# Attention scores from stacked fp16 halves that pass through DRAM, taken one iteration later, and the residual sum on GpSimd

## The chip, the cores and the metric

One NeuronCore of a Trainium2 chip runs the kernel. The time is that of one execution on the device, in microseconds (us). TensorE multiplies, VectorE and ScalarE work on tiles, GpSimd does small tile work and indirect transfers, SyncE starts most of the other transfers. Profile names: PE is TensorE's matmul, PEld its weight load, DVE is VectorE, ACT ScalarE, POOL GpSimd, SP SyncE; a q behind a name is that engine's own sequencer.

## The reference

The input x has 2 batches of 2048 tokens by 512. What is computed, cut to what matters:

```python
x = x + tanh(g_xattn[0]) * xattn(layernorm(x), ctx, ...)      # 16 heads of 32, 128 context rows
x = x + tanh(g_ffn[0]) * ffn(layernorm(x), ...)               # 8 experts of width 256, top 2, and a shared one of 512

q = query @ Wq.T + bq;  k = key @ Wk.T + bk;  v = value @ Wv.T + bv
att = einsum('bhsd,bhtd->bhst', q, k) / sqrt(32)              # masked by pad_mask and subsq_mask
out = einsum('bhst,bhtd->bhsd', softmax(att), v)
```

## The kernel before, in words

**Three passes.** Pass 1 takes 32 tiles of 128 tokens (tile n belongs to batch n % 2) through layernorm, query projection, attention, the residual sum, a second layernorm, the router and, for the tiles of batch 1, the shared expert. Pass 2 takes 71 slots of 128 gathered rows through the experts. Pass 3 sums everything up for the output and does the shared expert of batch 0. The change is in pass 1 and in what is set up ahead of it.

**The pipeline of pass 1.** Every engine has one `body(J, v)`, run once per iteration; iteration i is J = i // 2, v = i % 2. A stage with lag L works on tile i - L, and `tile(J, v, lag)` gives the tile n, its number j in its batch and its buffer u. The lags are LQ = 2 (transpose the normed tile, project it to q), LS = 3 (scores, row maxima, exp), LV = LS + 1 (probabilities transposed, times values), LX1 = LS + 2 (second half of the normalisation, residual sum, statistics), LX2 = LS + 3 (second layernorm, transpose, router), LR and LK for ranks and lists, and LU, LG, LD, LB for the shared expert, all counted from LX2. The order inside an iteration is the order in which `body` is written, engine by engine; semaphores tie the engines together. Work that belongs to no tile hangs on iteration numbers: weight peaks on DVE in iterations 3 to 14, and in iterations 16 to 31 the split of expert weights into fp16 halves, `split_high` on ACT when v = 0 and `split_low` on DVE (line 1097) when v = 1. PLAN_IT = NT + LK - 1 is the iteration in which DVE plans pass 2.

**Query projection.** x is split into an fp16 high and low half (`x_hi` on ACT, line 647; `x_lo` on DVE, line 942). `queries` (lines 1340 to 1342) makes q transposed, channels on partitions, in PSUM bank 0: four column blocks, each of 4 x 3 fp16 products over 128 rows. ACT then writes `q_t` in fp32 with four instructions that apply scale and bias (line 688) and raises `q_ready`, which releases bank 0 and the scores.

**Scores.** `scores(k)` (line 1301) is called for k = 0 and k = 2 and makes two groups of 4 heads each time, into banks 2 and 3. One head is one fp32 product over the 32 rows of that head; heads of row group g and g + 1 alternate. An fp32 product is two records in the trace, so 16 heads are 32 records a tile.

**Behind them.** DVE adds the mask and takes row maxima (`maxima(k)`, line 887) for four groups. GpSimd subtracts the maxima for three groups (`shift(k)`, line 527), ACT takes the exponentials (lines 629 and 681). PE transposes probabilities (`turn_probs`, line 1217), ACT copies them (`take_probs`, line 622), PE multiplies by values (`mix_values`, line 1325), DVE normalises (`normalise`, lines 899 and 901). DVE makes x1 = attn * gate + x (line 937), raising `x1_ready`; then statistics (line 951). `keys_and_values` in iteration 2 writes `k_t` and `vaug` (lines 867 and 872).

**GpSimd's order.** `shift(0)`, mask, `shift(1)`, mask, `shift(2)`, two small chains for the layernorms (lines 546 to 556), then two indirect transfers that scatter token numbers (line 565). **SP's order** in an iteration: store x1 (line 401), store the normed rows (line 405), load x (line 412), load x again for the residual (line 419), shared expert traffic.

## Time and profile before

| | |
|---|---|
| median of 3 runs | 1089.7 us (1083.06 to 1090.62) |
| the profiled execution's own time | 1085.73 us |
| its span in the profile | 1083.5 us |
| PE busy over the span | 93% |
| DVE busy | 72% |
| granted TensorE clock, mean over the span | 0.96 of full speed |

The span runs from the first to the last instruction that the profiler saw; the time of the execution has 2.2 us more around it. Pass 1 ends near 600 us. A busy share is an average over three passes with different limits, so the argument reads pass 1 by stretches. PE's records are pipelined: a matmul of 219 ns can be followed by the next one 56 ns later, so what an instruction costs PE is the distance between starts and not its own duration.

### The profile page before, as it was taken

To read this page: it belongs to the slowest core of one execution; us is meant where nothing else is said; L and a number is where in the kernel's file an instruction comes from. 1 tells how busy PE (TensorE), PEld (TensorE's weight loads), DVE (VectorE), ACT (ScalarE), POOL (GpSimd) and SP (SyncE) were. 2 spreads that over 40 slices of the span, in tenths; PEclk is the share of its full clock that TensorE was granted. 3 is DMA by queue.
4 is the path that set the end of the run, shared out by engine and by line. 5 is a ranking of instruction groups with operands and counts; after the bars stand their busy time and mean duration, and the time that the engine had idled before them with its cause. 6 is when DMAs were issued, how large, how long until landed. Compare 5 with 4: busy or idle time off the path is not lost.

```text
span 1083.5 us, 31212 instructions
## 1 busy us (share of the span) xinstructions
PE 1012.0 (93%) x10160; PEld 778.7 (72%) x10161; DVE 775.1 (72%) x2795; ACT 500.1 (46%) x1010; POOL 425.3 (39%) x606
## 2 busy tenths in 40 slices
PE   5889899999999999999996599999999999989997
PEld 4678889888899888899984355555555555578885
DVE  4577888887898888888776566666666666545656
ACT  2456555456566566666542344444444444311111
POOL 4333355454555565554533222222212221045553
PEclk9787899999999999999998799999999999999999
DMA  9502565742455433236225243333333334169987
GB/s 369 222 21 90 211 135 100 111 103 73 54 103 109 109 100 89 60 81 184 89 82 135 68 128 117 116 115 113 113 114 116 116 116 145 60 182 329 303 292 262
DMA packets 76754, 147.30 MB, mean 136 GB/s; under 512 B 20912, under 2 KB 23088, under 8 KB 73872
## 3 DMA queue, kind: packets, MB, share of 16 engines
q1 hardware_dynamic: 46800, 68.11, 25.4%
q0 software_dynamic: 12896, 35.58, 11.3%
q10 hardware_dynamic: 16992, 42.74, 10.2%
q8 instruction: 41, 0.67, 0.3%
q14 instruction: 25, 0.20, 0.1%
HBM read 94.04 MB, written 52.35 MB: 135 GB/s over the span
## 4 chain that ended last, share of the span: by engine, by line
PE 75%; DVE 9%; issue 6%; ACT 4%; DMA 3%; POOL 2%; another core or an unknown queue 1%; SPq 0%; ACTq 0%; POOLq 0%; DVEq 0%
PE bank L1217 10%; PE bank L1225 9%; PE bank L1226 9%; PE bank L1227 9%; PE bank L1325 8%; PE bank L1301 5%; PE bank L1275 5%; PE bank L1277 4%; PE bank L1276 4%; PE bank L1285 2%; PE bank L1342 2%; PE bank L1340 2%; PE bank L1341 2%; DVE arena L887 2%; PE bank L1287 2%
## 5 line engine op out<-in xcount | busy, mean ns | idle before, releaser
L1275 PE MATMUL bank<-arena,weights 128*128 128x128 f16 x1024 | 185.3, 225 | 13.5 <-DVE arena L1018 8.7
L1277 PE MATMUL bank<-arena,weights 128*128 128x128 f16 x1024 | 185.1, 225 | 0.0
L1276 PE MATMUL bank<-arena,weights 128*128 128x128 f16 x1024 | 185.1, 225 | 0.0
L1217 PE MATMUL bank<-ident,arena 128*128 128x128 f32 (+1 forms) x1336 | 179.5, 270 | 2.5 <-DMA arena<-normed_rows,arena 1.9
L579 POOL DMA_INDIRECT arena<-normed_rows,arena x71 | 69.1, 973 | 250.1 <-PE bank L1217 225.0
L1217 PEld LDWEIGHTS bank<-ident,arena 128*128 128x128 f32 (+1 forms) x1336 | 143.8, 141 | 23.8 <-DMA arena<-normed_rows,arena 2.5
L527 POOL TENSOR_TENSOR arena<-arena 128x512 f32<-128x512 f32 x96 | 101.0, 1052 | 142.7 <-DVE arena L887 135.1
L1325 PE MATMUL bank<-arena 128*128 128x33 f32 x1024 | 137.3, 280 | 7.6 <-ACT arena L622 7.6
L1325 PEld LDWEIGHTS bank<-arena 128*128 128x128 f32 x1024 | 131.4, 200 | 14.7 <-ACT arena L622 12.2
L887 DVE CUSTOM_DVE_ANT_0 arena<-bank,arena 128x128 f32<-128x128 f32 x512 | 116.9, 284 | 31.2 <-PE bank L1301 31.2
L622 ACT ACTIVATE arena<-bank 128x512 f32<-128x512 f32 x128 | 75.9, 593 | 115.5 <-PE bank L1217 108.2
L1275 PEld LDWEIGHTS bank<-arena,weights 128*128 128x128 f16 x1024 | 103.4, 101 | 21.1 <-DVE arena L1018 8.8
L1225 PE MATMUL bank<-weights,arena 128*128 x284 | 107.7, 379 | 1.7 <-DVE arena L1153 1.6
L1226 PE MATMUL bank<-weights,arena 128*128 x284 | 107.6, 379 | 0.0
L1227 PE MATMUL bank<-weights,arena 128*128 x284 | 107.6, 379 | 0.0
L1276 PEld LDWEIGHTS bank<-arena,weights 128*128 128x128 f16 x1024 | 103.5, 101 | 2.0
L1277 PEld LDWEIGHTS bank<-arena,weights 128*128 128x128 f16 x1024 | 103.7, 101 | 0.0
L1340 PE MATMUL bank<-arena 128*128 128x128 f16 x512 | 93.9, 227 | 3.0 <-issue 1.6
L1159 DVE TENSOR_SCALAR arena<-bank,arena,w_back 128x512 f32<-128x512 f32 x71 | 57.5, 810 | 54.2 <-PE bank L1227 54.2
L1341 PE MATMUL bank<-arena 128*128 128x128 f16 x512 | 93.8, 227 | 1.1 <-issue 1.1
L1342 PE MATMUL bank<-arena 128*128 128x128 f16 x512 | 93.6, 227 | 0.0
L1301 PE MATMUL bank<-arena 32*128 32x128 f32 x1024 | 78.9, 295 | 9.4 <-ACT arena L688 7.5
(196 smaller groups left out, 2268.9 us busy)
## 6 DMA issues: line engine op xcount, KB each, us to landing
expert_rows<-arena ACTq DMA_DIRECT2D x71, 256.0 KB, 2.2
arena<-in_x SPq DMA_DIRECT2D x64, 256.0 KB
x_rows<-arena SPq DMA_DIRECT2D x48, 256.0 KB, 5.4
arena<-x_rows SPq DMA_DIRECT2D x48, 256.0 KB, 3.8
weights<-in_w_gu ACTq DMA_DIRECT2D x8, 1024.0 KB, 7.0
normed_rows<-arena SPq DMA_DIRECT2D x32, 256.0 KB, 5.6
out<-weights ACTq DMA_DIRECT2D x32, 256.0 KB, 4.5
weights<-in_w_down ACTq DMA_DIRECT2D x4, 1024.0 KB, 13.5
```

What stands on the lines that cost most here:

```text
L887: last = d.tensor_tensor_reduce(score[u][:, hh * T:(hh + 1) * T], bank[2 + k % 2][:, h * T:(h + 1) * T], mask_bias[u], 1.0, LOWEST, ALU.ad ...
L1217: last = t.transpose(dst[:, c * P:(c + 1) * P], src[:, c * P:(c + 1) * P], (ident16 if src.dtype == F16 else ident)[:, :])
L1225: t.matmul(dst, hi[:, rows], w_hi(c), start=(c == 0), stop=False)
L1226: t.matmul(dst, hi[:, rows], w_lo(c), start=False, stop=False)
L1227: last = t.matmul(dst, lo[:, rows], w_hi(c), start=False, stop=(c == chunks - 1))
L1275: t.matmul(at, shared(c, part, 0, dc), x_hi_c, start=(c == 0), stop=False)
L1276: t.matmul(at, shared(c, part, 0, dc), x_lo_c, start=False, stop=False)
L1277: last = t.matmul(at, shared(c, part, 1, dc), x_hi_c, start=False, stop=(c == EC - 1))
L1301: mm = t.matmul(bank[2 + g % 2][:, c * T:(c + 1) * T], q_t[u][rows, c * P:(c + 1) * P], k_t[rows, c, u, :], start=True, stop=True)
L1325: last = t.matmul(bank[A_BANK][:, at:at + D + 1], probs_t[k % 2][:, h * P:(h + 1) * P], vaug[:, u, k * HG + h, :], start=True, stop=True)
L1340: t.matmul(dst, wq[:, 0, at:at + P], x_hi[:, xs], start=(ci == 0), stop=False)
L1341: t.matmul(dst, wq[:, 0, at:at + P], x_lo[:, xs], start=False, stop=False)
```

## The change

It does these things:

- q is no longer written in fp32. ACT writes the fp16 high half of q, scaled (`q_halves`), straight from bank 0, and DVE writes the low half at the start of the next iteration, which is now what raises `q_ready`. SP stores both halves to DRAM (`query_halves`) and, once that has landed, loads them back as `q_stack`: for each head 96 rows, high, low, high.
- The keys go the same way once, in iteration 2, with rows high, high, low, and with a scale that is found from their largest value by `top_peaks`, `all_peaks` and `scale_of`.
- A head's score is one fp16 product over the 96 rows. `scores` makes one group of 4 heads per call and is called four times, (0) and (1) at the place of the old (0), (2) and (3) at that of the old (2). The scale goes into the exponentials.
- bq is added on PE: a fp16 product over 64 rows, `bq_half` by `bias_row`, closes each of the four column blocks of `queries`.
- LS becomes 4, so all later stages come one iteration later.
- The attention gate is multiplied into the values and their bias once, so x1 is a plain sum, and it is made on GpSimd at the start of the iteration, ahead of `shift(0)`.
- SP's order in an iteration: store q, load x twice, store x1, load the stack, store the normed rows.
- Arena addresses move, two semaphores are merged into one at the layernorm and in pass 2, and load_down(1) is issued in iteration NT + 2.

```diff
-        LQ, LS = 2, 3
+        LQ, LS = 2, 4
@@ SP, body
+                n, j, u = tile(J, v, LQ + 1)
+                if live(n, NT):
+                    hold(sp, sp_passed, (q_ready, n + 1))
+                    sp.dma_start(q_dram[u].rearrange("a p n -> p a n"), q_halves.rearrange("p (a n) -> p a n", a=2)).then_inc(q_out[u], 16)
...
+                n, j, u = tile(J, v, LQ + 1)
+                if live(n, NT):
+                    hold(sp, sp_passed, (q_out[u], 16 * (j + 1)))
+                    hold(sp, sp_passed, (s_done, group(n - 2, EC - 1)))
+                    stack(q_stack[u], q_dram[u], (0, 1, 0), q_stacked[u])
...
+            def stack(dst, src, parts, done):
+
+                for at, part in enumerate(parts):
+                    sp.dma_start(dst[at * D:(at + 1) * D, :].rearrange("d (h n) -> d h n", h=HG),
+                                 src[part].rearrange("(h d) n -> d h n", h=HG)).then_inc(done, 16)
...
+                if it == KEYS_IT:
+                    sp.wait_ge(k_lo_set, 1)
+                    sp.dma_start(k_dram.rearrange("a p n -> p a n"), k_halves.rearrange("p (a n) -> p a n", a=2)).then_inc(k_out, 16)
+                    sp.wait_ge(k_out, 16)
+                    stack(k_stack, k_dram, (0, 0, 1), k_stacked)
@@ GpSimd, body
+                n, j, u = tile(J, v, LX1)
+                if live(n, NT):
+                    hold(pool, pool_passed, (res_here[u], 16 * (j + 1)))
+                    need(pool, x1_out[u], 16 * j)
+                    need(pool, xn2_ready, n - 1)
+                    pool.wait_ge(attn_done[0], n + 1)
+                    pool.wait_ge(attn_done[1], n + 1)
+                    g.tensor_tensor(x1[u], attn, x_res[u], ALU.add).then_inc(x1_ready, 1)
@@ ACT, body
-                    need(act, s_done, group(n - 2, EC - 1))
-                    for c in range(EC):
-                        last = a.activation(q_t[u][:, c * P:(c + 1) * P], bank[0][:, c * P:(c + 1) * P], ACT.Identity,
-                                            scale=w_back[:, 0:1], bias=bq_s[:, c:c + 1])
-                    last.then_inc(q_ready, 1)
+                    hold(act, act_passed, (q_out[(v - LQ - 1) % 2], 16 * (j + u)))
+                    a.activation(q_halves[:, 0:E], bank[0][:, :], ACT.Copy, scale=Q_DOWN).then_inc(q_hi_ready, 1)
@@ DVE, normalise and body
+                        need(dve, x1_ready, n)
...
+                n, j, u = tile(J, v, LQ + 1)
+                if live(n, NT):
+                    dve.wait_ge(q_hi_ready, n + 1)
+                    d.scalar_tensor_tensor(q_halves[:, E:2 * E], bank[0][:, :], Q_DOWN, q_halves[:, 0:E], ALU.mult, ALU.subtract).then_inc(q_ready, 1)
...
-                    d.scalar_tensor_tensor(x1[u5], attn, gate[:, 0:1], x_res[u5], ALU.mult, ALU.add).then_inc(x1_ready, 1)
@@ PE, body
-                        for c in range(EC):
-                            for g in (k, k + 1):
-                                rows = slice(g * D, (g + 1) * D)
-                                mm = t.matmul(bank[2 + g % 2][:, c * T:(c + 1) * T], q_t[u][rows, c * P:(c + 1) * P],
-                                              k_t[rows, c, u, :], start=True, stop=True)
+                        pe.wait_ge(q_stacked[u], 16 * PARTS * (j + 1))
+                        pe.wait_ge(k_stacked, 16 * PARTS)
+                        need(pe, max_done, group(n, k - 2))
+                        for h in range(HG):
+                            q_at, k_at = (h * EC + k) * P, ((h * EC + k) * B + u) * T
+                            last = t.matmul(bank[2 + k % 2][:, h * T:(h + 1) * T], q_stack[u][0:STACK, q_at:q_at + P],
+                                            k_stack[0:STACK, k_at:k_at + T], start=True, stop=True)
+                        last.then_inc(s_done, 1)
...
-                                last = t.matmul(dst, wq[:, 1, at:at + P], x_hi[:, xs], start=False, stop=(ci == EC - 1))
+                                t.matmul(dst, wq[:, 1, at:at + P], x_hi[:, xs], start=False, stop=False)
+                            last = t.matmul(dst, bq_half[:, co * P:(co + 1) * P], bias_row[:, :], start=False, stop=True)
```

How the order moves is shown at two places. First TensorE in a late iteration of pass 1, at the second call for scores and at the projection. In the kernel before, L1217 is a transpose, L1301 a score, L1285 the shared expert and L1340 to L1342 the projection:

```order
L1217 MATMUL bank<-ident,arena 128x128 x3
L302 REGISTER_ALU [waits q_ready]
L1301 MATMUL bank<-arena 128x128 [waits max_done]
L1301 MATMUL bank<-arena 128x128 x7
L1285 MATMUL bank<-weights,arena 128x512
```

In the changed kernel at the same place L1365 is a score and L1351 the shared expert; further on, L1404 to L1406 are the projection and L1407 is the bias:

```order
L1365 MATMUL bank<-arena 128x128 [waits max_done]
L1365 MATMUL bank<-arena 128x128 x3
L317 REGISTER_ALU [waits k_stacked,q_stacked1]
L1365 MATMUL bank<-arena 128x128 [waits max_done]
L1365 MATMUL bank<-arena 128x128 x3
L1351 MATMUL bank<-weights,arena 128x512
...
L1404 MATMUL bank<-arena 128x128
L1405 MATMUL bank<-arena 128x128
L1406 MATMUL bank<-arena 128x128
L1407 MATMUL bank<-bias_row,bq_half 128x128
L1404 MATMUL bank<-arena 128x128
```

The count of products stays 8 here and 16 a tile, their wait on `q_ready` has become one on the transfer, and a bias product stands between the column blocks of the projection, four times a tile.

Second GpSimd, at the seam between two iterations. Before, L562 and L565 are the token scatter, L527 is `shift`, L537 the mask:

```order
L562 COPY arena<-token_no 128x1 [waits rows_out0]
L565 DMA token_of_row<-arena 36864x1 [waits row_ready,tok_ready]
L565 DMA token_of_row<-arena 36864x1
L527 TENSOR_TENSOR arena<-arena 128x512 [waits max_done]
L537 TENSOR_TENSOR arena<-arena,pad_keep 128x128 [waits max_done,sub_set]
```

In the changed kernel L611 and L614 are the scatter, L577 is the residual sum and L568 is `shift`:

```order
L611 COPY arena<-token_no 128x1 [waits rows_out1]
L614 DMA token_of_row<-arena 36864x1 [waits row_ready,tok_ready]
L614 DMA token_of_row<-arena 36864x1
L577 TENSOR_TENSOR arena<-arena 128x512 [waits attn_done0,xn2_ready,attn_done1,x1_out1,res_here1]
L568 TENSOR_TENSOR arena<-arena 128x512 [waits max_done]
```

The sum with its five waits stands between the scatter of the iteration before and `shift(0)`.

## Rows read from the trace of the kernel before

**Rows 1.** The page: busy time of each engine, and TensorE's granted clock in 40 slices

```profile
PE 1012.0 (93%) x10160; PEld 778.7 (72%) x10161; DVE 775.1 (72%) x2795; ACT 500.1 (46%) x1010; POOL 425.3 (39%) x606
PEclk9787899999999999999998799999999999999999
```

**Rows 2.** Stretches of pass 1: start, end, length, busy us by engine, clock, DMA, GB/s

```profile
45.00:64.00 19.00, 18.98 (x133) 17.66 (x131) 8.62 (x42) 7.45 (x17) 5.68 (x9) 0.55 0.35 136
399.00:414.80 15.80, 15.78 (x223) 15.03 (x222) 14.00 (x64) 9.20 (x21) 7.07 (x10) 1.00 0.37 99
414.80:431.00 16.20, 15.80 (x188) 13.64 (x188) 12.89 (x69) 11.14 (x22) 10.46 (x18) 1.00 0.30 93
550.00:600.00 50.00, 33.42 (x389) 27.78 (x388) 36.72 (x157) 14.82 (x28) 16.78 (x25) 0.88 0.43 107
```

**Rows 3.** Groups by line over the span: busy us, mean ns, idle before and releaser

```profile
L1301 PE MATMUL bank<-arena 32*128 32x128 f32 x1024 | 78.9, 295 | 9.4 <-ACT arena L688 7.5 <-DVE arena L887 1.5
L688 ACT ACTIVATE arena<-bank,bq_s,w_back 128x128 f32<-128x128 f32 x128 | 47.9, 455 | 13.4 <-PE bank L1342 13.3
L937 DVE SCALAR_TENSOR_TENSOR arena<-arena,gate 128x512 f32<-128x512 f32 x32 | 38.9, 1216 | 1.2
L942 DVE SCALAR_TENSOR_TENSOR arena<-bank,arena 128x512 f16<-128x512 f32 x32 | 22.0, 686 | 17.1 <-ACT arena L647 17.1
```

**Rows 4.** Timeline of PE around both score calls of one iteration: start, length

```profile
414.14 0.63 PE L1217 MATMUL bank<-ident,arena 128*128 128x128 f32 x4
415.91 0.23 PE L1275 MATMUL bank<-arena,weights 128*128 128x128 f16 x1
415.98 0.22 PE L1276 MATMUL bank<-arena,weights 128*128 128x128 f16 x1
416.14 0.22 PE L1276 MATMUL bank<-arena,weights 128*128 128x128 f16 x1
421.28 0.49 PE L1217 MATMUL bank<-ident,arena 128*128 128x128 f32 x3
421.70 1.16 PE L1301 MATMUL bank<-arena 32*128 32x128 f32 x16
421.70 0.38 PE L1301 MATMUL bank<-arena 32*128 32x128 f32 x2
422.79 0.39 PE L1285 MATMUL bank<-weights,arena 128*128 128x512 f16 x1
```

**Rows 5.** Waits of PEld from 60 to 550 us

```profile
PEld bank L1301 <- ACT arena L688: 7.4, 13, 2.9
```

**Rows 6.** Timeline of DVE, ACT and POOL at one place of the loop, and an earlier L937

```profile
413.19 1.49 ACT L688 ACTIVATE arena<-bank,bq_s,w_back 128x128 f32<-128x128 f32 x4
415.19 0.42 DVE L901 TENSOR_TENSOR arena<-bank,arena 128x256 f32<-128x256 f32 x1
420.08 1.05 POOL L527 TENSOR_TENSOR arena<-arena 128x512 f32<-128x512 f32 x1
401.71 1.05 POOL L527 TENSOR_TENSOR arena<-arena 128x512 f32<-128x512 f32 x1
402.00 1.73 DVE L937 SCALAR_TENSOR_TENSOR arena<-arena,gate 128x512 f32<-128x512 f32 x1
418.07 0.75 DVE L937 SCALAR_TENSOR_TENSOR arena<-arena,gate 128x512 f32<-128x512 f32 x1
```

**Rows 7.** DMA issues: count, KB each, median us to landing

```profile
x_rows<-arena SPq DMA_DIRECT2D x48, 256.0 KB, 5.4
weights<-in_w_down ACTq DMA_DIRECT2D x4, 1024.0 KB, 13.5
```

**Rows 8.** Timeline: the keys on DVE, and the first scores of the first two tiles

```profile
26.25 1.64 DVE L867 TENSOR_SCALAR arena<-bank,bk_s 128x256 f32<-128x256 f32 x4
33.68 1.16 PE L1301 MATMUL bank<-arena 32*128 32x128 f32 x16
44.78 1.82 PE L1301 MATMUL bank<-arena 32*128 32x128 f32 x16 [1.86 <-ACT arena L688]
```

More of the change, by code:

```diff
@@ L680, in body @@
                         sc = score[u][:, h * T:(h + 1) * T]
-                        last = a.activation(sc, sc, ACT.Exp, bias=peaks_neg[:, h - H + HG:h - H + HG + 1])
+                        last = a.activation(sc, sc, ACT.Exp, scale=score_scale[:, :], bias=peaks_neg[:, h - H + HG:h - H + HG + 1])
                     last.then_inc(exp_done, 1)
@@ L1249, in _, with values @@
             last.then_inc(kv_mm, 1)
-            def values():
+            def values(b):
                 pe.wait_ge(v_in, 16)
-                for b in range(B):
-                    for ci in range(EC):
-                        last = t.matmul(bank[6 + b][:, :], ctx_s[:, ci, b * T:(b + 1) * T], wv_s[:, ci, :],
-                                        start=(ci == 0), stop=(ci == EC - 1))
-                last.then_inc(kv_mm, 1)
+                for ci in range(EC):
+                    last = t.matmul(bank[6 + b][:, :], ctx_s[:, ci, b * T:(b + 1) * T], wv_s[:, ci, :],
+                                    start=(ci == 0), stop=(ci == EC - 1))
+                if b == B - 1:
+                    last.then_inc(kv_mm, 1)
             def it_is_first(n, k):
```

264 lines of the change are left out of this document (153 added, 111 removed).

## The prediction

> **What bounds the kernel now.** I read the page first, for busy shares and clock, then pass 1 by stretches, then the groups by line, then the timeline around the changed places, and last the waits and the transfers.
>
> The page has PE busy for 93% of the span and DVE for 72% [rows 1]. That says little of where a saved microsecond counts, so I go to stretches. In a late stretch of the loop two iterations take 15.80 and 16.20 us, PE is busy for 15.78 and 15.80 us of them at full clock, DVE for 14.00 and 12.89, ACT for 9.20 and 11.14, GpSimd for 7.07 and 10.46 [rows 2]. PE bounds the loop there, and what it saves per tile is saved from the iteration, as long as DVE does not take over about 2 us lower. Early in pass 1 it is mixed: from 45 to 64 us PE is busy all the time at a granted clock of 0.55, about its lower level of 1.2 GHz, and the clock slices 2 to 7 of the page are below full [rows 1, 2]. At the end of the pass, from 550 to 600 us, PE is busy 33.42 of 50 us [rows 2]: the pipeline drains through chains of small steps.
>
> **Scores on PE.** What counts is the distance between starts. In a late iteration the last fp32 pass ahead of the second score call begins at 421.28 + 0.49 - 0.27 = 421.50 (a pass is recorded for 0.27), and the first product behind the call at 422.79: 1.29 us, of which 0.11 is that pass's own distance, so the call takes 1.18 [rows 4]. The first call is from 414.14 + 0.63 - 0.27 = 414.50 to 415.91, 1.41 less 0.11, or 1.30. Together 2.48 us a tile; the group agrees, 78.9 us over 32 tiles is 2.47 [rows 3]. The fp16 products are 0.055 apart (415.98 to 416.14 is three of them) [rows 4], and 128 columns over 96 rows are the same stream, so 16 heads take 0.89. Scores alone save 1.59 us a tile.
>
> **The bias on PE.** Four products more a tile are 0.22 us if they stream like the others. But they are products over 64 rows between products over 128, and no such product is in this trace. The nearest row is the switch to the scores' 32 rows. Going in, the last pass starts at 421.50 and the first score at 421.70, 0.20 where passes are 0.11 apart: 0.09 lost. The first scores are recorded for 0.38 where the rest have about 0.28, another 0.10. Coming out, the last pass starts at 421.70 + 1.16 - 0.27 = 422.59 and the next product at 422.79, again 0.20 and 0.09 lost [rows 4]. A visit thus costs 0.28 over its stream. If a visit of 64 rows costs the same, the bias takes 4 x (0.28 + 0.055) = 1.34 us a tile. Lower bound 0.22, no cost of switching. Upper bound: the 0.20 is a fixed gap whatever streams, then 4 x (0.20 + 0.10 + 0.20 - 0.055) = 1.78. I take 1.34, since the loss over the stream is what the row shows both ways. The Trainium skill, TensorEngine Tiling (Array Packing), Key Properties, says that changing the tiling mode drains TensorE. The trace agrees as far as it goes: the loss is there on entry and on exit of the 32-row scores. By that rule this change takes 2 score visits away and puts 4 bias visits in; without it the bias would be 0.22.
>
> PE per tile: -2.48 + 0.89 + 1.34 = -0.25 us; bounds -1.37 and +0.19. The loop is bound by PE as in rows 2 for some 18 iterations (those of 16 to 33), so -4 us, bounds -25 and +3.
>
> **The early iterations (4 to 15).** The same per tile, at a clock that is partly half, and PE or DVE waits in turn. There q's way over ACT goes from the path: PEld waited 7.4 us for L688 in 13 places from 60 to 550 us, most of them early [rows 5], and ACT's four instructions, 47.9 us over 32 tiles [rows 3], or 1.5 a tile, become one copy of about 0.6. DVE gives up L937, 38.9 us in all at 1.216, and takes q's low half, priced by L942 at 0.686 [rows 3]: 17 us less busy, half a microsecond a tile, and DVE is near the bound there. I take -8 us together; bounds 0 (the waits return on another semaphore) and -20 (7.4 of waits, 12 iterations at 0.5 of DVE, the rest PE at the lower level).
>
> **The residual sum on GpSimd.** One more instruction like L527, 1.05 us [rows 6]. It stands ahead of `shift(0)` and behind the scatter, and everything on GpSimd behind it moves back by 1.05 when it is late: the exponentials, the mask, and x1_ready with the store of x1 and SP's queue behind that. In the row, `shift(0)` starts at 420.08 [rows 6], so the sum would end near 421.1; statistics need it only behind `maxima(2)`, near 424. GpSimd is busy 10.46 of 16.20 at most [rows 2]; I cost it at nothing, covered by PE's 15.8. If that cover is gone it costs up to 1.05 an iteration. L937 was 1.73 us when it began beside an L527 (401.71 to 402.76) and 0.75 alone [rows 6]. The Trainium skill, SBUF — State Buffer, on the two sides of ports, has this as an exclusive lock between a GpSimd operation and a DVE operation with two SBUF inputs; the row agrees. By it the new sum can hold up DVE operations that read two SBUF tiles (the weight split), by 1 us each time at most; the removed L937 was the one that met it.
>
> **The stack through DRAM.** ACT's q starts at 413.19 and would be done at 413.8; DVE comes to q's low half behind L901, at 415.61, and ends at 416.3 [rows 3, 6], with L942 as the price. The store is priced by x_rows, 256 KB in 5.4 us [rows 7], to 421.7. Behind it on SP wait the stack's three loads, then the store of normed rows. The loads are 384 KB in rows of 1 KB; at 5.4 us plus 0.7 for issuing three they land near 427.8. The first scores of the next iteration start one iteration after 414.82, near 430.8. So the transfers fit with about 3 us to spare, and cost nothing in the loop. Bounds: 0, and where 1 MB loads run (13.5 us to landing [rows 7], iterations 7 to 11) some 8 us late, two or three times.
>
> **Start and the extra iteration.** Before, the keys were made at 26.25 to 27.9 and the first scores ran at 33.68, the second tile's at 44.78 [rows 8]. Now the keys need a reduction, a transpose and a spread on PE, the scale, a high half on ACT and a low half on DVE: I estimate ready at about 36. A store and a load of 5.4 each put the keys in place at 47, and q's first stack, which SP issues behind them, at about 50. The first scores then run in iteration 4 at about 50, where before the second tile's ran at 44.78. The work of that iteration is one stage lighter, so this is not 16 us but 50 - 44.8 plus PE's own 2.4 of scores not yet done, less what PE can do meanwhile: +6, bounds 0 and +12. At the other end one iteration more drains. It holds no new work, PE is idle a third of the time there [rows 2]: +3, bounds +1 and +8.
>
> **Sum.** -4 - 8 + 6 + 3 = -3 us against the profiled execution's 1085.73, so 1083. That execution lies 4 us under the median of the runs shown, 1089.7, which others are compared with; on that scale I forecast 1087. Passes 2 and 3 have only addresses and semaphores changed: 0. All lower bounds together would be -44 (-25, -20, 0, +1), all upper ones +43 (+3, 0, +20 for late stacks, +12, +8); neither is likely.
>
> **The rivals.** (A) The 64-row products stream without a loss. For: accumulation goes on in the same bank and the row shown is of 32 rows in alternating groups. Against: both edges of those rows lose. PE then saves 1.37 a tile: 18 x 1.37 = 25, early -13 (the 8 above, and 12 iterations at 1.12 more of which four tenths count), start and drain +9: -29, 1060. It also needs DVE to keep up, with 14.00 - 0.5 of about 14.6 us. (B) Slower: the stack is late. Its place is `scores(0)` on PE, which then waits for a transfer. From q's high half to the landed stack takes 14 us against 17 us to the next scores, and it decides from the point where store and load take 3 us more than priced, by 1 KB rows, by SP being held at x1_ready behind GpSimd's scatter, or by other transfers. Were it 4 us more in all iterations, 1 us x 30 = 30 less overlap of some odd ones, say +22: 1109. For: three transfers in series and a queue that waits in order. Against: the DMA engines' share is 0.30 to 0.37 in rows 2. (C) The switch costs the upper bound: +0.19 instead of -0.25, 0.44 x 30 = +13: 1100. (D) GpSimd's sum, shift and ACT's exponentials become the ring that closes the loop: GpSimd is idle a third of the time, so at most +0.5 an iteration: 1102 or so.
>
> **Chances.** Forecast 0.36, A 0.25, B 0.17, C 0.14, D 0.08. This measurement can tell about 1% from no change. Of the forecast 0.29 lies within 1%, 0.05 under it and 0.02 over; A is faster; B is slower; C and D are half within 1%, half slower. That gives faster 0.30, same 0.40, slower 0.30. The range must take in A and B: 1056 to 1108. The forecast's own range is 1075 to 1098.
>
> **What would show it.** A score group of 512 records at 0.055 apart, about 0.9 us a tile. Around each bias product: the distance from the product before it to the one behind it, 0.39 if I am right, 0.11 in rival A, 0.50 or more in C. Pairs of late iterations of 31.5 us instead of 32.0; 29.3 in A. PE waiting for a transfer ahead of the scores would be B, GpSimd's sum as what ACT's exponentials wait for would be D. First scores near 50 us. I am wrong if late iterations keep or gain time for a reason other than PE's switches, or if pass 1 ends more than 10 us off 597.

## The result, and the profile after

The changed kernel takes 1130.97 us, median of 4 runs (1128.83 to 1134.22). The kernel before takes 1086.64 in its 4 runs beside it. The ratio is 1.041, with a 95% interval of 1.036 to 1.046: 4% slower, outside the forecast range and slower than any rival. Ratios here and below are formed from the fast runs alone, which leaves out four of the seven runs of before in the second group and four of the 23 in the fourth, so the medians given there do not yield them.

The page after, as [rows 1] for before: busy time by engine, and the granted clock in 40 slices.

```profile
PE 1020.4 (90%) x9779; PEld 774.0 (69%) x9780; DVE 791.4 (70%) x2809; ACT 496.5 (44%) x915; POOL 470.8 (42%) x643
PEclk9877699999999999999997799999999999999999
```

PE has 381 records fewer and is still busy 8 us longer. To see where the 45 us of span come in, I put marks into pass 1: the first row maximum on DVE, the last one, and the last addition into `seen`, which ends the pass. Timeline of DVE in the kernel before:

```profile
34.99 0.28 DVE L887 CUSTOM_DVE_ANT_0 arena<-bank,arena 128x128 f32<-128x128 f32 x1
...
551.55 0.28 DVE L887 CUSTOM_DVE_ANT_0 arena<-bank,arena 128x128 f32<-128x128 f32 x1
...
589.97 0.15 DVE L926 TENSOR_TENSOR seen<-seen,arena 128x8 f16<-128x8 f16 x1
```

And after:

```profile
57.32 0.29 DVE L961 CUSTOM_DVE_ANT_0 arena<-bank,arena 128x128 f32<-128x128 f32 x1 [5.77 <-PE bank L1365]
...
590.80 0.29 DVE L961 CUSTOM_DVE_ANT_0 arena<-bank,arena 128x128 f32<-128x128 f32 x1
...
634.15 0.15 DVE L1005 TENSOR_TENSOR seen<-seen,arena 128x8 f16<-128x8 f16 x1
```

The start is 22.3 us longer (57.3 against 35.0), the 32 tiles from first to last maximum take 16.9 more (533.5 against 516.6), the tail 4.9 (43.3 against 38.4). That makes 44.2, and passes 2 and 3 add 1. These are marks and not three causes: by DVE's statistics of the input tiles the pass is 5.8 us longer up to the sixteenth tile, 18.7 from there to the last, and 19.7 behind it.

**What PE does per tile came out better than forecast.** Two score calls of four heads and one bias product in a late iteration, timeline of PE after:

```profile
404.22 0.61 PE L1365 MATMUL bank<-arena 96*128 96x128 f16 x8
404.67 0.22 PE L1341 MATMUL bank<-arena,weights 128*128 128x128 f16 x1
...
410.56 0.22 PE L1406 MATMUL bank<-arena 128*128 128x128 f16 x1
410.71 0.23 PE L1407 MATMUL bank<-bias_row,bq_half 64*128 64x128 f16 x1
410.87 0.23 PE L1404 MATMUL bank<-arena 128*128 128x128 f16 x1
```

Eight scores take 0.45 us, so a tile 0.90, as forecast. Around the bias product it is 0.31 from the product before to the one behind, where I forecast 0.39 and rival A 0.11. So PE saves 2.48 - 0.90 - 4 x (0.31 - 0.055) = 0.56 us a tile.

**Yet late iterations are longer.** Stretches of eight late iterations, from DVE's statistics of one input tile to those of the eighth behind it (start, end, length, busy us of PE, PEld, DVE, ACT, POOL, clock). Before:

```profile
381.10:508.80 127.70, 125.90 (x1634) 114.58 (x1634) 107.45 (x526) 81.34 (x173) 70.02 (x108) 1.00 0.40 101
```

After:

```profile
396.20:533.30 137.10, 127.90 (x1543) 114.78 (x1542) 109.24 (x525) 80.44 (x149) 82.54 (x116) 0.96 0.56 124
```

An iteration went from 15.96 to 17.14 us. PE was idle 1.8 us in the eight, now 9.2, and its clock is no longer full. The waits of that stretch after:

```profile
PE bank L1388 <- ACT arena L679: 9.2, 6, 2.1
```

L1388 is `mix_values`, L679 `take_probs`. One such wait is followed back in the timelines. GpSimd after, from the end of one iteration into the next:

```profile
430.95 0.22 POOL L601 TENSOR_SCALAR arena<-arena 128x1 f32<-128x1 f32 x1 [1.68 <-DVE arena L1080]
...
433.25 1.10 POOL L614 DMA_INDIRECT token_of_row<-arena  x1 [0.85 <-POOL arena L611]
434.67 0.96 POOL L614 DMA_INDIRECT token_of_row<-arena  x1 [0.31 <-issue]
435.66 1.27 POOL L577 TENSOR_TENSOR arena<-arena 128x512 f32<-128x512 f32 x1
436.88 1.04 POOL L568 TENSOR_TENSOR arena<-arena 128x512 f32<-128x512 f32 x1
```

ACT after, behind it:

```profile
437.95 0.72 ACT L686 ACTIVATE arena<-arena,score_scale 128x512 f32<-128x512 f32 x1 [2.18 <-POOL arena L568]
...
438.92 1.99 ACT L804 ACTIVATE weights<-weights,w_scale  x1
440.81 0.71 ACT L686 ACTIVATE arena<-arena,score_scale 128x512 f32<-128x512 f32 x1
441.43 0.58 ACT L679 ACTIVATE arena<-bank 128x512 f32<-128x512 f32 x1
```

And PE:

```profile
442.06 1.08 PE L1388 MATMUL bank<-arena 128*128 128x33 f32 x8 [2.06 <-ACT arena L679]
```

Read it as one chain: DVE's last statistics of an iteration release GpSimd (430.95), which makes the scale of the layernorm, scatters twice, makes the sum and only then the shift; that releases ACT's first exponential, behind which stand the weight split, the second exponential and, in ACT's order, `take_probs(2)` of the tile before; PE needs that for `mix_values(2)`, and everything DVE does later in the iteration hangs on PE. The sum lies in this chain with its full 1.27 us.

The chain was there before, which I had overlooked. The chain of waits of the kernel before, from 380 to 394 us, start and length of each step:

```profile
387.19 0.97 POOL token_of_row L565
388.18 1.06 POOL arena L527
...
390.24 1.46 ACT weights L747
...
392.03 0.61 ACT arena L629
392.65 0.49 ACT arena L622
393.19 1.08 PE bank L1325 x8
```

It had hardly any slack: PE waited for L622 four times in the eight iterations, 1.6 us in all. That GpSimd was idle 5.74 of 16.20 us [rows 2] said nothing of what this chain could take in.

**Idle PE can cost twice.** Between 463.2 and 498.8 us PE waited once, 2.06 us ahead of 475.54. Stretches around this gap, after:

```profile
472.00:475.50 3.50, 1.48 (x23) 1.24 (x20) 3.32 (x30) 3.50 (x7) 2.59 (x5) 1.00 0.94 172
475.50:479.00 3.50, 3.46 (x21) 3.40 (x22) 1.76 (x6) 1.09 (x3) 0.45 (x1) 0.51 0.70 203
479.00:482.50 3.50, 3.50 (x32) 2.88 (x30) 1.41 (x3) 2.70 (x6) 1.16 (x4) 0.51 0.00 0
482.50:486.00 3.50, 3.50 (x54) 3.15 (x52) 1.12 (x3) 1.37 (x3) 2.38 (x3) 1.00 0.01 0
```

The clock goes from full to 0.51, about the 1.2 GHz level, for 7 us in which PE is busy, and back. These two iterations took 35.6 us; the two before them, with gaps of 2.06 and 0.60 and no fall of the clock, 33.5. So one gap of this length was followed by a fall and one was not, and these rows do not show what decides it.

### The profile page after: what moved, and what is told of

It is laid out like the page before. It is cut to its first block, busy times and chain, and to the rows that moved or that the text cites. A ratio compares the mean times of both kernels' runs of the same rounds, so it can differ in the third digit from the quotient of the medians.

```text
span 1128.8 us, 31111 instructions
## 1 busy us (share of the span) xinstructions
PE 1020.4 (90%) x9779; PEld 774.0 (69%) x9780; DVE 791.4 (70%) x2809; ACT 496.5 (44%) x915; POOL 470.8 (42%) x643
## 4 chain that ended last, share of the span: by engine, by line
PE 71%; DVE 8%; DMA 6%; issue 6%; POOL 4%; ACT 3%; SPq 1%; ACTq 0%; DVEq 0%; POOLq 0%; another core or an unknown queue 0%
PE bank L1283 9%; PE bank L1388 8%; PE bank L1291 8%; PE bank L1292 8%; PE bank L1293 8%; PE bank L1341 4%; PE bank L1343 4%; PE bank L1342 4%; PE bank L1404 3%; PE bank L1405 2%; PE bank L1406 2%; PE bank L1351 2%; PE bank L1352 2%; PE bank L1353 2%; PE bank L1365 2%
## 5 line engine op out<-in xcount | busy, mean ns | idle before, releaser
L1283 PE MATMUL bank<-ident,arena 128*128 128x128 f32 (+1 forms) x1336 | 182.2, 272 | 4.6 <-DVE arena L989 2.2
L1342 PE MATMUL bank<-arena,weights 128*128 128x128 f16 x1024 | 185.8, 226 | 0.0
L1388 PE MATMUL bank<-arena 128*128 128x33 f32 x1024 | 142.4, 285 | 34.9 <-ACT arena L679 29.4
L1388 PEld LDWEIGHTS bank<-arena 128*128 128x128 f32 x1024 | 133.6, 202 | 46.8 <-ACT arena L679 38.6
L568 POOL TENSOR_TENSOR arena<-arena 128x512 f32<-128x512 f32 x96 | 101.7, 1060 | 92.0 <-DVE arena L961 91.8
L679 ACT ACTIVATE arena<-bank 128x512 f32<-128x512 f32 x128 | 75.8, 592 | 134.9 <-PE bank L1283 124.0
L1404 PE MATMUL bank<-arena 128*128 128x128 f16 x512 | 107.5, 240 | 3.9 <-DVE arena L1015 3.7
L1405 PE MATMUL bank<-arena 128*128 128x128 f16 x512 | 107.0, 239 | 0.0
L1406 PE MATMUL bank<-arena 128*128 128x128 f16 x512 | 106.8, 239 | 0.0
L1342 PEld LDWEIGHTS bank<-arena,weights 128*128 128x128 f16 x1024 | 103.9, 101 | 2.1
L686 ACT ACTIVATE arena<-arena,score_scale 128x512 f32<-128x512 f32 x96 | 69.1, 720 | 68.5 <-POOL arena L568 68.5
```

What stands on the lines that cost most here:

```text
L1283: last = t.transpose(dst[:, c * P:(c + 1) * P], src[:, c * P:(c + 1) * P], (ident16 if src.dtype == F16 else ident)[:, :])
L1342: t.matmul(at, shared(c, part, 0, dc), x_lo_c, start=False, stop=False)
L1388: last = t.matmul(bank[A_BANK][:, at:at + D + 1], probs_t[k % 2][:, h * P:(h + 1) * P], vaug[:, u, k * HG + h, :], start=True, stop=True)
L1404: t.matmul(dst, wq[:, 0, at:at + P], x_hi[:, xs], start=(ci == 0), stop=False)
L1405: t.matmul(dst, wq[:, 0, at:at + P], x_lo[:, xs], start=False, stop=False)
L1406: t.matmul(dst, wq[:, 1, at:at + P], x_hi[:, xs], start=False, stop=False)
```

## The experiments

Fifteen kernels. Medians of before differ from chip to chip (1091, 1120, 1089 and 1130 us for the four groups below), so kernels are compared by their ratio to before on the same chip. The changed kernel itself ran only beside the before of 1086.64, so its 1.041 is set against ratios of other chips. Where a ratio cannot tell, I use the end of pass 1 in the one profiled execution (590.0 before, 634.2 after). That is a single execution, and the four runs of rows_later_sum lie 15 us apart. The chips themselves differ behind pass 1 above all: passes 2 and 3 took 491 to 497 us in the traces of the first and third group and 514 to 531 in those of the others, while probs_first_before ended pass 1 at 592.1 on the chip where before takes 1130.

### First group: one part of the change each

**lag_only** adds to before nothing but the extra iteration.

```diff
-        LQ, LS = 2, 3
+        LQ, LS = 2, 4
@@ SP: the mask's load goes from lag 0 to lag LS - 3
```

> The kernel before with LS = 4 and nothing else (the load of the mask moves with it). Theory 1 (the extra iteration is paid whole): an iteration at each end is nearly its full length of about 15 us, so 1087 + 10 to 20, about 1101, and late pairs of iterations stay near 31.9 us. Rival (the forecast's own pricing: the iteration holds no new work, +3 to +5): 1091. A second rival, that the shift by one of the shared expert's work against the weight split is what costs: late pairs grow to 33 or more and the time is near 1115.

Measured: ratio 1.0135 (1.0102 to 1.0167), 15 us: theory 1. So the extra iteration alone is worth five times my 3 us. Its eight late iterations take 124.60 us, less than before. The cost lies elsewhere. The whole of pass 1, lag_only:

```profile
0.00:611.30 611.30, 559.04 (x6507) 505.19 (x6508) 459.53 (x2155) 327.75 (x689) 298.14 (x453) 0.92 0.49 117
```

Before:

```profile
0.00:590.00 590.00, 547.42 (x6507) 493.30 (x6509) 463.25 (x2155) 326.16 (x689) 285.58 (x452) 0.95 0.46 121
```

The same 6507 records of PE take it 11.6 us more, and it is idle 9.7 us more. (The profiled execution was the slowest of the four, 4 us over their median, so it shows 21 us where the median has 15.) The added iteration stands behind the last input tile. From that tile's statistics to the end of the pass, before:

```profile
508.80:590.00 81.20, 73.27 (x890) 63.44 (x890) 58.66 (x294) 38.07 (x82) 35.29 (x51) 0.96 0.41 114
```

And lag_only:

```profile
507.70:611.30 103.60, 92.03 (x1059) 81.54 (x1058) 68.97 (x355) 44.63 (x96) 42.86 (x62) 0.88 0.44 118
```

That is 22.4 us more, with 169 records more, 3.6 us more of idle PE and a clock of 0.88 instead of 0.96. Ahead of it the gains and losses cancel: up to the sixteenth input tile lag_only is 12 us quicker, from there to the last 11 slower. Two of its gaps, of 3.9 us up to 185.2 and of 3.4 up to 291.9, have no release that the profile names, and the clock was at half for 5 us behind the first and 14 behind the second. Whether they belong to the extra iteration is open.

**sum_dve** takes the changed kernel and puts the sum back on DVE, where it was.

```diff
@@ GpSimd
-                    g.tensor_tensor(x1[u], attn, x_res[u], ALU.add).then_inc(x1_ready, 1)
@@ DVE, ahead of maxima(1)
+                    d.scalar_tensor_tensor(x1[u5], attn, 1.0, x_res[u5], ALU.mult, ALU.add).then_inc(x1_ready, 1)
```

> The changed kernel with the residual sum on VectorE at its old place. Theory 1 (the loop is closed by a chain of GpSimd's scatter, the sum, shift(0), ScalarE's exponential, the weight split's high half, the next exponential and take_probs(2), for which TensorE waits ahead of mix_values(2)): 1.3 us leaves that chain in each pair of iterations and the VectorE operation that lasted 2.45 us beside the sum returns to 0.7, so a late pair falls from 33.5 to near 31.5 us and the time to about 1131 - 16 - some early gain = 1112. Rival (TensorE's own work or the transfers set the pace): within 3 us of 1131.

Measured: 1.019 (1.0148 to 1.0232), 1110.33 us, theory 1: half of the whole loss goes away with one instruction a tile. Its eight late iterations:

```profile
388.70:515.70 127.00, 122.33 (x1538) 110.36 (x1538) 109.76 (x534) 80.21 (x148) 69.76 (x108) 1.00 0.59 134
```

PE is 3.6 us less busy than before and 4.7 idle instead of 1.8, of which it waits 3.5 for `take_probs`; for the other 1.2 the profile names no release. Most of what the scores save is lost in the same wait, and the iteration is nearly as long as before.

**bias_128** pads the bias product from 64 to 128 rows with zeros, so its stream and its result are the same.

```diff
-        bq_half = sb("bq_half", [2 * D, E], F16)
+        bq_half = sb("bq_half", [P, E], F16)
@@ the same for bq_raw, bias_row and the host's zero rows
```

> The changed kernel with the bias product over 128 rows, 64 of them zero, so that TensorE keeps one tiling mode. The distance around a bias product falls from 0.31 to 0.11 us, 0.8 us a tile. Theory 1 (in the late loop TensorE waits once per pair for a chain that does not hold the bias): of the 26 us that come off TensorE in 32 tiles less than half shows, 1131 to 1120. Rival (TensorE sets the pace everywhere): 1105.

Measured: 1.0293 (1.0253 to 1.0332), theory 1: some 13 of the 26 us that PE no longer spends show. Timeline of PE in bias_128:

```profile
405.18 0.22 PE L1406 MATMUL bank<-arena 128*128 128x128 f16 x1
405.23 0.22 PE L1407 MATMUL bank<-bias_row,bq_half 128*128 128x128 f16 x1
405.29 0.22 PE L1404 MATMUL bank<-arena 128*128 128x128 f16 x1
```

Now it is 0.11 from product to product across the bias, against 0.31. So the loss of 0.20 a visit is that of going from 128 rows to 64 and back, and it costs nothing to avoid. The Trainium skill, TensorEngine Tiling (Array Packing), Key Properties, says that changing the tiling mode drains TensorE. The rows agree: 0.31 us around the product over 64 rows, 0.11 around the padded one.

**late_split** moves ACT's weight split of every second iteration behind `take_probs(3)`.

```diff
-                elif v == 0:
-                    split_high(J)
                 exponent(1)
                 take_probs(2)
...
                 take_probs(3)
+                if not isinstance(J, int) and v == 0:
+                    split_high(J)
```

> The changed kernel with ScalarE's high half of the weight split (1.99 us, once in each of 8 pairs of iterations) issued behind take_probs(3) instead of ahead of the second exponential. Theory 1 (that instruction stands in the chain TensorE waits for): TensorE's wait of 2 us ahead of mix_values(2) goes, 8 pairs fall from 33.5 to about 31.7 us, 1131 - 14 = 1117. Rival (the wait only moves, to take_probs(3) or to VectorE's low half): 1131 within 3.

Measured: 1.0347 (1.0305 to 1.0389), not told apart from the changed kernel for certain: the rival. The chain of waits of late_split shows why:

```profile
458.44 1.28 POOL arena L577
...
462.21 1.05 POOL arena L568
...
463.92 0.59 ACT arena L679
```

With the split gone from between the exponentials, ACT waits for GpSimd's second shift instead. The chain goes one step further along GpSimd. Eight late iterations of this trace take 132.0 us against 137.1, with 4.2 us of waits for `take_probs` and 3.0 for row maxima, so the split did stand in the way there; yet its pass 1 ends at 638.2, later than the changed kernel's 634.2, and I did not follow where the rest went.

### Second group: do the parts add, where in the chain, and the start

On this chip before took 1119.69 us (1103 to 1124), and intervals are wide.

**sum_dve_bias** is sum_dve and bias_128 together.

> The changed kernel with two edits at once: the sum of attention and x back on DVE where it was, and the bias product over 128 rows. Alone the first gave 1110.3 and the second 1121.3, against 1131.0. Theory 1 (the sum keeps ACT's exponentials and so PE waiting, the bias costs PE its switches; two separate costs): the gains add, some 20.6 + 9.7, so 1101, late pairs of iterations near 30.9 us (31.8 less four products that lose 0.2 each, in two tiles). Theory 2 (with PE 0.8 us a tile quicker, the chain over GpSimd, ACT and PE closes the loop again): 1107 to 1110, late pairs stay at 31.6 or more with PE waiting longer for ACT's take_probs.

Measured: 1.0164 (0.999 to 1.034); pass 1 ends at 611.0, sum_dve's at 615.5. Eight late iterations take 126.5 us against 127.0, and PE waits 6.7 us for `take_probs` instead of 3.5: theory 2. Much of the 0.8 us a tile that the bias no longer costs goes into the wait.

**sum_later** keeps the sum on GpSimd and puts it behind `shift(0)`.

```diff
+                shift(0)
                 n, j, u = tile(J, v, LX1)
                 if live(n, NT):
...
                     g.tensor_tensor(x1[u], attn, x_res[u], ALU.add).then_inc(x1_ready, 1)
-                shift(0)
```

> The changed kernel with the sum still on GpSimd, but behind shift(0) instead of ahead of it. Theory 1 (its place in GpSimd's order is what costs: 1.3 us ahead of the shift that ACT's first exponential waits for): most of the 21 us come back, 1114 to 1119, late pairs near 32.0. Theory 2 (what costs is that it shares the way to the tiles with DVE, whose instructions beside it take 2 us longer, wherever it stands): 1125 to 1135, late pairs 33 or more.

Measured: 1.0471 (1.032 to 1.063), pass 1 ends at 633.3: nothing gained that can be told. Here my two theories were badly cut. The instructions of DVE beside the sum are no longer stretched (L998 took 1.56 us in the mean of four in late iterations of the changed kernel, 0.684 in each of them here), and still nothing is gained. The timeline of GpSimd in sum_later has the reason, as in late_split: the sum now stands ahead of the second shift, and that one is waited for as well.

```profile
455.40 1.05 POOL L568 TENSOR_TENSOR arena<-arena 128x512 f32<-128x512 f32 x1
456.40 1.28 POOL L578 TENSOR_TENSOR arena<-arena 128x512 f32<-128x512 f32 x1
...
459.02 1.04 POOL L568 TENSOR_TENSOR arena<-arena 128x512 f32<-128x512 f32 x1
```

**pool_sum_before** is the kernel before with the sum on GpSimd ahead of `shift(0)`, otherwise as it was. It leaves out the gate on the attention.

> The kernel before with one part of the change alone: the sum of attention and x as a plain sum on GpSimd ahead of shift(0), off DVE. The gate on the attention is left out. Theory 1 (the chain GpSimd, ACT, PE already stood in the chain of waits of before, so 1.3 us more in it come out as time whatever the scores cost): 1100 to 1112, late pairs of 33 to 33.5 instead of 31.9. Theory 2 (only because PE has become quicker per tile does the sum cost): 1087 to 1095, late pairs of 32.0 to 32.4.

Measured: 1.0228 (1.007 to 1.039); pass 1 ends at 611.4, 21 us later than before's, and eight late iterations, from 387.4 to 523.8, take 136.4 us against 127.7. So the sum costs about this much with no other part of the change present: theory 1.

**keys_late** stores the keys' halves four times in a row in the changed kernel.

```diff
-                    sp.dma_start(k_dram.rearrange("a p n -> p a n"), k_halves.rearrange("p (a n) -> p a n", a=2)).then_inc(k_out, 16)
-                    sp.wait_ge(k_out, 16)
+                    for again in range(4):
+                        sp.dma_start(k_dram.rearrange("a p n -> p a n"), k_halves.rearrange("p (a n) -> p a n", a=2)).then_inc(k_out, 16)
+                        sp.wait_ge(k_out, 16 * (again + 1))
```

> The changed kernel with the store of the keys' halves issued and waited for four times in a row instead of once, which puts the keys' stack, and the first queries' stack behind it, some 8.5 us later (one store took 2.85 us from issue to the next). Theory 1 (what the start loses passes through to the end): first scores near 65 us instead of 56.7 and 1138 to 1140. Theory 2 (PE does the waiting iteration's other work meanwhile and the early iterations take the loss up): under 1134.

Measured: 1.0568 (1.043 to 1.070). The first row maximum comes at 68.7 instead of 57.3, 11.4 later, and pass 1 ends at 648.4 instead of 634.2, 14.2 later. What the start loses passes through: theory 1.

### Third group: the chain opened on GpSimd's side

All four move the two scatters of a tile's rows from the end of an iteration to behind `shift(2)` of the next one; the last tile's stay.

```diff
+                def put_rows(lag, now):
+                    n, j, u = tile(J, v, lag)
+                    if now and live(n, NT):
...
                 shift(2)
+                put_rows(LK + 1, not (isinstance(J, int) and SPAN1 * J + v == PLAN_IT + 1))
...
-                n, j, u = tile(J, v, LK)
-                if live(n, NT):
...
-                        g.indirect_dma_start(list_dram, bass.IndirectOffsetOnAxis(ap=row_i[at][:, k:k + 1], axis=0),
-                                             tok_i[at], None).then_inc(rows_out[u], 16)
+                put_rows(LK, SPAN1 * J + v == PLAN_IT if isinstance(J, int) else False)
```

**rows_later** does this to the changed kernel.

> The changed kernel, nothing taken out, but GpSimd's two scatters of a tile's rows stand one iteration later behind shift(2) instead of at the iteration's end (the last tile's stay). In the chain of waits they, with what issuing them takes, are some 4 us between DVE's last statistics and the sum with shift(0). Theory 1 (one queue: statistics, scatters, sum, shift, exponential, take_probs, PE; the sum costs because it lengthens this chain): the chain is 3 to 4 us shorter, the waits of PE for take_probs go, late pairs 31.0 to 31.5 and a ratio of 1.015 to 1.022, as with the sum on DVE. Theory 2 (the sum costs because DVE's instructions beside it run longer, or by memory traffic): late pairs stay at 33 or more and the ratio at 1.035 to 1.045.

Measured: 1.0121 (1.0067 to 1.0175), against 1.041. With the sum still on GpSimd, at least as much comes back as by taking it away. Eight late iterations of rows_later:

```profile
382.20:506.60 124.40, 122.47 (x1536) 110.08 (x1536) 107.86 (x525) 80.62 (x148) 81.98 (x117) 1.00 0.54 137
```

15.55 us an iteration instead of 17.14, and PE waits 1.9 us for `take_probs` instead of 9.2: theory 1.

**rows_later_before** does it to the kernel before.

> The kernel before with the scatters one iteration later behind shift(2), nothing else. Theory 1: before stood just at the edge (PE waited 1.6 us in eight iterations for take_probs), so pairs go from 31.9 to 31.2 and the ratio is 0.988 to 0.997. Theory 2: no gain, 0.998 or more.

Measured: 1.0108 (1.006 to 1.016), slower than before. Theory 1 is wrong here. The whole of its pass 1:

```profile
0.00:608.20 608.20, 560.13 (x6506) 504.45 (x6508) 461.13 (x2154) 326.93 (x689) 287.38 (x452) 0.92 0.45 117
```

PE is idle 5.5 us more than in before, and 12.7 us longer busy with the same records, at 0.92 of the clock instead of 0.95. The six runs agree: their mean granted clock is 0.945 to 0.956, that of the 11 runs of before 0.951 to 0.964. Eight late iterations take 132.3 us, 4.6 more than before, and one pair of them makes the difference: it takes 37.2, the other three 31.2 to 32.5. Timeline of ACT in the long pair:

```profile
400.17 0.60 ACT L651 ACTIVATE arena<-bank 128x512 f16<-128x512 f32 x1 [3.38 <-remote]
```

ACT stood 3.38 us here for something that the profile does not name, and GpSimd had made two shifts by then (395.00 and 397.71). PE waited 2.03 us for `take_probs` behind it, up to 404.57, and the clock was at half from 404.6 to 411.5. So in this pair it was ACT that kept PE and not the chain over GpSimd, and the lower clock followed. What held ACT, and whether it does so in the other runs, stays open.

**rows_later_sum** is pool_sum_before with the scatters moved; it leaves out the gate too.

> The kernel before with the sum alone on GpSimd (which gave 1.023 and ended pass 1 some 21 us later) and the scatters one iteration later. The gate on the attention is left out again. Theory 1: the sum now fits in what the scatters left free, and the ratio falls to 0.99 to 1.003. Theory 2: it stays at 1.015 to 1.025.

Measured: 1.0101 (1.005 to 1.015). My range was too low, as rows_later_before has shown, but beside that one (1.0108) the sum on GpSimd now costs nothing that can be measured (some 0.007 either way), where it cost 0.023 with the scatters in the chain.

**rows_later_all** is the changed kernel with sum_dve, bias_128 and the scatters moved.

> The changed kernel with the sum on DVE, the bias over 128 rows and the scatters one iteration later: what is left of the change is the scores as one product, through DRAM, and one iteration more. Theory 1: the chain over GpSimd no longer keeps PE waiting, so that PE's saving a tile comes out: late pairs 29.8 to 30.3 (two tiles, 1.59 saved in the scores less the bias of 0.22 each, from 31.2 in the kernel before with the chain open), some 12 us less in the second half of the pass than before, against about 15 for the extra iteration and 8 at the start: ratio 1.000 to 1.010. Theory 2 (DVE bounds next, busy 27.4 us of a pair and its own waits): late pairs over 30.8 and a ratio of 1.012 or more.

Measured: 1.0111 (1.0065 to 1.0156). Its eight late iterations:

```profile
380.40:498.20 117.80, 115.86 (x1537) 109.17 (x1536) 110.52 (x534) 79.12 (x149) 72.73 (x109) 1.00 0.61 145
```

14.7 us an iteration, 1.2 less than before: this is what the scores are worth once nothing stands in their way. Yet pass 1 ends at 604.9. The first row maximum is at 60.8, 25.8 later than before; the 32 tiles take 16.1 less; the tail takes 5 more. Theory 2 is wrong in its size, though DVE, busy 110.5 of 117.8 us, is now near to bounding the loop, and the ratio lies just over theory 1's 1.010.

Some 10 us of this pass are rival B, once. Timeline of PE in rows_later_all:

```profile
532.56 0.93 PE L1367 MATMUL bank<-arena 96*128 96x128 f16 x7 [4.64 <-DMA arena<-query_halves]
```

PE waited 4.64 us for a stack, the clock was at half from 530.9 to 541.2, and this pair of iterations took 39.1 us by the statistics of x1, where the four before it took 26.4 to 30.2. So even with the chain open the transfer is not free in every iteration; whether it comes late in the other runs no trace shows.

### Fourth group: the chain opened on ACT's side

All three swap two lines of ACT.

```diff
-                exponent(1)
                 take_probs(2)
+                exponent(1)
```

**probs_first** does it to the changed kernel.

> The changed kernel with two lines of ACT swapped: take_probs(2) of the older tile ahead of exponent(1) of the newer one, whose shift it then need not wait for. Theory 1 (this order is the link by which GpSimd holds PE): PE no longer waits 13 us for take_probs from 270 to 540 us, late pairs of 30.9 to 31.8 instead of 33.5, and a ratio of 1.010 to 1.022. Theory 2 (the chain closes through another link, exponentials to transposes or maxima, just as long): late pairs stay at 33 or more and the ratio at 1.03 or more.

Measured: 1.0214 (1.0143 to 1.0286), against 1.041. In the one trace, eight late iterations take 135.5 us, with 5.8 us of waits for `take_probs` instead of 9.2 and a clock of 0.96. Pass 1 ends at 623.8 instead of 634.2. So by the ratio half of the loss goes by this link alone, but the late pairs that theory 1 wanted are not in the trace, and part of the chain closes in another way, which I did not follow.

**probs_first_before** does it to the kernel before.

> The kernel before with the same two lines swapped. Theory 1 (an open chain is a gain, and the moved scatters were what cost before 1.1%): late pairs of 31.1 to 31.3 and a ratio of 0.985 to 0.998. Theory 2 (an open chain gains nothing in before, since PE is busy either way and the middle of the pass is set by the granted clock): 0.999 to 1.012.

Measured: 0.9969 (0.9937 to 1.0000), with eight late iterations of 125.5 us against 127.7 and no wait left. An open chain is a small gain, at the edge of what can be told, and rows_later_before's loss came with moving the scatters and not with opening the chain.

**probs_first_all** is the changed kernel with sum_dve, bias_128 and the swap.

> The changed kernel with the sum on DVE, the bias over 128 rows and the two lines of ACT swapped; GpSimd's scatters stand where they were. Theory 1: late pairs near 29.4 as with the scatters moved, and a ratio of 1.000 to 1.011: the start 22 us later and the iteration more, some 15, are not made up by 1.2 us a tile. Theory 2 (swapping only trades one wait for another): late pairs over 31 and a ratio over 1.012.

Measured: 1.0037 (0.9998 to 1.0076), with eight late iterations of 121.6 us and the end of pass 1 at 607.8. This is the best form of the change that I have, and it is not faster than before. No version here beats before by more than its interval.

## Why the prediction was wrong, step by step

**Scores on PE: right.** 0.90 us a tile against 0.89 forecast.

**The bias on PE: right in kind, a third too high.** A visit costs 0.31 against 0.39; 1.02 us a tile, not 1.34. Rivals A (0.11) and C (0.50 or more) fell, and bias_128 shows that it is what 128 rows give.

**"I cost it at nothing, covered by PE's 15.8": this step failed first.** The sum on GpSimd is worth 0.022 of the time (sum_dve), 0.023 in the kernel before (pool_sum_before), the largest part of those that were taken alone. The forecast took a busy share for slack. Rival D named the ring, with "at most +0.5 an iteration" because "GpSimd is idle a third of the time"; late iterations gained 1.2 us, two and a half times that, since the sum enters with all its 1.27 us and PE's waits take the clock down. The late loop's -4 (PE's saving) is therefore about +20: 18 x 1.2 = 21.

**"Extra iteration +3, it holds no new work": failed.** It is 15 us (lag_only), outside my bound of 8. No new work is no reason for a short iteration: the stretch behind the last input tile took 103.6 us instead of 81.2, at a clock of 0.88.

**Start +6: failed, outside its bound of 12.** The first scores ran at 56.67, forecast 50. SP's transfers after:

```profile
40.75 0.39 SPq L472 DMA_DIRECT2D key_halves<-arena  x1
...
49.38 1.26 SPq L457 DMA_DIRECT2D arena<-query_halves  x3
```

The keys were ready at 40.7, not 36: `spread_peaks(2)` stands on PE behind the values of batch 0 (31.75 to 36.88). The queries' stack was issued near the 50 at which I had it landed, and landed 7 us later. The worse error was the discount: I counted 50 - 44.8 because the iteration has less to do. The second tile's scores were 20.7 us late too (65.45 against 44.78), and keys_late shows that such a delay reaches the end whole.

**Early iterations -8: not seen, within its bounds.** From the first row maximum to the last the tiles took 16.9 us more, of which the last 16 iterations hold 18.7 (276.1 us from the sixteenth input statistics to the last, 257.4 before), which leaves about -2.

**The stack through DRAM in the loop: as forecast, almost free.** From 57 us on PE waited for a stack 2.6 us in all, and rival B fell for this kernel. With the chain open it came up once, for 4.6 us (rows_later_all).

**DVE's instructions stretched beside the sum: there, and not the cause.** Timelines of DVE and of GpSimd after:

```profile
416.43 2.45 DVE L998 SCALAR_TENSOR_TENSOR arena<-arena 128x512 f16<-128x512 f16 x1
```

```profile
417.03 1.28 POOL L577 TENSOR_TENSOR arena<-arena 128x512 f32<-128x512 f32 x1
```

An instruction of DVE with two SBUF inputs takes 2.45 us beside the sum and 0.684 in sum_later, where the loss stays. The Trainium skill, SBUF — State Buffer, SBUF: two separate sides, calls the port pair that GpSimd and such an instruction share an exclusive lock. The rows agree in that L998 ends 0.57 us behind the sum; that the one which starts first keeps the ports, as the page also has it, they do not show, since L998's record starts 0.6 us ahead of the sum's. It decides nothing here.

The parts, each taken alone: iteration 0.0135, sum 0.022, bias 0.012, together 0.047, against 0.041 for the whole. That the two are near each other proves nothing, since two parts are missing: the later start beyond lag_only's (18.7 us, 0.017) on the one side and the scores' saving on the other. The scores' saving, 1.6 us a tile, shows only in kernels whose chain is open, and there the start and the iteration eat it. These prices depend on each other: the scatters moved (0.029) and the sum taken away (0.022) are two ways to open the same chain.

Two things were luck or loose. All upper bounds together come to 1087 + 43 = 1130, beside the measured 1131, but by other terms: 20 of the 43 were for late stacks, which cost 2.6. And the sign "more than 10 us off 597" came from a pass that ends near 600; it ends at 590.0, so the forecast meant 587, and the pass ended 47 us later.

What stays open: why moving the scatters costs before 1.1%, what the gaps without a named release in lag_only are, and which link keeps half of the loss in probs_first.

## What to carry to other kernels

An engine that is idle a third of the time has no slack if its work between two hand-overs lies in a chain that is as long as the iteration. Before moving an instruction onto such an engine, follow the chain of waits once round the loop in the profile of before, and ask what stands behind the new instruction in its queue and in the queue of the engine that waits. An added pipeline stage is to be priced as a whole iteration, as it was here, and a later first product as lost in full, unless an experiment shows otherwise.

## What the runs showed of the hardware

A gap of 2.06 us in PE's work was followed by 7 us at half the clock (0.51), while another one of 2.06 us, ahead of 442.06, was not. Over pass 1 the same 6506 or 6507 records kept PE busy for 547 us at a mean clock of 0.95 in two kernels (before, probs_first_before), for 550 at 0.93 in a third (rows_later_sum), and for 559 to 561 at 0.92 in three others (lag_only, pool_sum_before, rows_later_before). In those three PE was also idle 5.5 to 9.7 us longer than in before. But in rows_later_sum it was idle 1.6 us less and busy 2.6 us longer, so the sum of PE's idle time does not settle its clock.

A product over 64 rows between products over 128 cost 0.20 us more than its stream; padded with zeros to 128 rows it cost its stream, 0.055.
